# A layer norm between two graph layers, moved from node-major to feature-major

## The reference, cut to what matters

```python
# layer 0, relational: per edge h[src] * norm, summed by (type, dst), times W_rel
W_rel = jnp.einsum('rb,bdf->rdf', w_comp, weight)
agg = jax.ops.segment_sum(h[src] * norm, etype * n_nodes + dst, n_rels * n_nodes)
node_repr = einsum('rnd,rdf->nf', agg, W_rel) + h_bias + h @ loop_weight   # then relu
x = _layernorm(x + _L0_gnn_ref(...))       # (x - mean) / sqrt(var + eps), over 128 features
# layer 1: per edge
e = (x[dst] - x[src]) @ theta_w.T + x[src] @ phi_w.T
e = relu(bn(e)) @ fc1_w.T ;  e = relu(bn(e))
x = _layernorm(x + relu(segment_mean(e, dst) + x))
```

## Time and profile before

| | us |
|---|---|
| median of 3 runs | 3459.71 |
| lowest, highest | 3441.71, 3469.89 |
| the profiled execution, its time | 3434.9 |
| its span | 3433.1 |
| busy PE, DVE, ACT, POOL | 2137.0, 1219.2, 698.3, 1869.4 |
| mean granted PE clock, share of full | 0.719 |

### The profile page before, as it was taken

How to read it: one execution, slowest core, us unless ns; L and a number is a source line. 1 busy time by engine, 2 the same in 40 slices (tenths; PEclk the granted TensorE clock), 3 DMA queues, 4 the chain that set the end, 5 groups by cost and what they waited for, 6 DMA issues and landing times. The chain is left out here.

```text
span 3433.1 us, 51738 instructions
## 1 busy us (share of the span) xinstructions
PE 2137.0 (62%) x11161; PEld 1666.7 (49%) x11162; DVE 1219.2 (36%) x3285; ACT 698.3 (20%) x1046; POOL 1869.4 (54%) x2429
## 2 busy tenths in 40 slices
PE   3665666666666655455455554565555579799992
PEld 2555555556566544233333333333333333599991
DVE  3333333333343355233333332333333367411116
ACT  2111111111111121000000000010000045566661
POOL 5665666666666601555555555555555500499990
PEclk9788777877777867555655555555555599999995
DMA  5122211222122103222222222232222267433331
GB/s 120 50 55 53 54 52 51 57 56 52 52 55 57 46 7 110 71 84 83 83 82 82 82 82 82 82 96 83 75 90 85 78 252 277 157 134 134 134 122 38
DMA packets 120501, 300.17 MB, mean 87 GB/s; under 512 B 34397, under 2 KB 71282, under 8 KB 101632
## 3 DMA queue, kind: packets, MB, share of 16 engines
q1 hardware_dynamic: 63216, 145.36, 12.7%
q0 software_dynamic: 50176, 102.86, 11.7%
q10 hardware_dynamic: 7056, 51.38, 3.8%
HBM read 235.97 MB, written 63.51 MB: 87 GB/s over the span
## 5 line engine op out<-in xcount | busy, mean ns | idle before, releaser
L568 POOL DMA_INDIRECT G<-btab,ix x784 | 739.5, 943 | 639.6 <-POOLq L56 422.9
L554 POOL DMA_INDIRECT G<-in_x,srcT x784 | 746.5, 952 | 461.8 <-issue 230.3
L725 PE MATMUL PS<-BIG,onesb 2*128 2x512 bf16 x196 | 109.8, 560 | 640.5 <-PEq L56 361.6
L659 PE MATMUL PS<-BIG 128*128 128x192 f32 x1568 | 354.2, 373 | 140.1 <-issue 139.6
L650 PE MATMUL PS<-BIG,G 128*128 128x192 f32 x1568 | 366.1, 396 | 85.1 <-PEq L56 41.7
L1274 DVE TENSOR_SCALAR ohT<-PS,node_col 80x512 bf16<-80x512 f32 x196 | 146.1, 745 | 705.8 <-DVEq L56 512.2
L659 PEld LDWEIGHTS PS<-BIG 128*128 128x128 f32 x1568 | 309.6, 221 | 173.1 <-issue 173.1
L734 PE MATMUL PS<-ident,G 128*128 128x128 f32 x1568 | 376.6, 416 | 16.4 <-issue 11.6
L650 PEld LDWEIGHTS PS<-BIG,G 128*128 128x128 f32 x1568 | 333.7, 239 | 100.8 <-issue 99.9
L594 POOL TENSOR_SCALAR BIG<-iota_w,BIG 128x80 f32<-128x80 f32 x784 | 360.7, 481 | 18.6 <-POOLq L56 15.7
L900 ACT ACTIVATE BIG<-PS 128x512 f32<-128x512 f32 x196 | 117.0, 597 | 1220.5 <-ACTq L56 733.2
(11 more groups left out here) (168 smaller groups left out, 1910.1 us busy)
## 6 DMA issues: line engine op xcount, KB each, us to landing
BIG<-spill SPq DMA_DIRECT2D x98, 1024.0 KB, 4.7
spill<-BIG ACTq DMA_DIRECT2D x49, 1024.0 KB
G<-in_x,srcT POOLq DMA_INDIRECT x784
G<-btab,ix POOLq DMA_INDIRECT x784
typ_i<-in_edge_type SPq DMA_DIRECT2D x97, 128.0 KB
BIG<-atab SPq DMA_DIRECT2D x196, 60.0 KB
atab<-BIG SPq DMA_DIRECT2D x13, 384.0 KB, 2.6
btab<-bst SPq DMA_DIRECT2D x13, 256.0 KB, 2.3
```

What stands on the lines that cost most here:

```text
L554: nc.gpsimd.indirect_dma_start(out=G[:, g % 2, t, :], out_offset=None, in_=x, in_offset=bass.IndirectOffsetOnAxis(ap=srcT[:, TPG * g + t:T ...
L568: nc.gpsimd.indirect_dma_start(out=G[:, h, t, :], out_offset=None, in_=rows_of, in_offset=bass.IndirectOffsetOnAxis(ap=ix[:, h, t:t + 1], ...
L659: mm = pe.matmul(PS[:, 4 + p, 0:TPP * TWIN], basis[:, b, :], zs[:, p, :, b, :], start=(b == 0), stop=(b == B - 1), skip_group_check=True)
```

## The change

The norm is done unit by unit and feature-major. Since layer norm is (x - mean) times a number r for each node, and taking the mean off is a product with a constant matrix, B = r * (x C W) for C = identity - 1/128. The kernel makes `ctab` once, the constant C beside both weights times C, and for each unit PE multiplies the feature-major residual by it: that gives centred x and centred B; ACT squares and sums the first for the variance and scales the second by r. The last unit has two windows instead of four. All of B is made and stored before A. POOL waits for B's stores alone. x is loaded window by window in the first pass and kept transposed in `X`'s place; the bias goes in with the loop product. `steps_lo` and `steps_hi` move to another PSUM bank. A root activation stands at ACT's beginning. (Declarations are cut.)

```diff
 SP
-            sp.wait_ge(rows_used, 1)
-            sp.dma_start(X[:, 0:NW - 1, :], x[0:(NW - 1) * TNODES, :].rearrange("(w p) d -> p w d", p=P)).then_inc(x_in, 16)
-            sp.dma_start(X[0:LASTN, NW - 1, :], x[(NW - 1) * TNODES:N, :]).then_inc(x_in, 16)
-            with sp.Fori(1, NC - 1) as c:
-                take(sp, typ_free)
-                load_types(c, [ROW] * TPC)
...
+            def first_pass(g, h, use):
+                take(sp, xw_free)
...
+                    sp.dma_start(xn[:, h, 0:D], x[bass.ds(g * TNODES, TNODES), :]).then_inc(x_in[h], 16)
+                    if h == 0:
+                        take(sp, typ_free)
...
+                            load_types(use + 1, [ROW] * TPC)
...
-            def store_tables(u, s, use):
...
-            sp.sem_inc(tabs_done, 1)
+            def store_b(u, s, use):
+                n = len(windows_of(u))
                 take(sp, bst_ready)
...
+            by_pairs(sp, NBU, store_b)
+            def store_a(u, s, use):
+                n = len(windows_of(u))
                 take(sp, ast_ready)
...
+            by_pairs(sp, NBU, store_a)
 POOL
-            by_pairs(pool, NBU, keep)
-            pool.wait_ge(tabs_done, 1)
+            pool.wait_ge(bst_out[0], 16 * (NBU - NBU // 2))
+            pool.wait_ge(bst_out[1], 16 * (NBU // 2))
             gathers(btab[:, :])
 PE
+            pe.matmul(PS[:, 5, 0:2 * D], center[:, :], thph[:, :], start=True, stop=True).then_inc(cw_ps, 1)
...
-                    take(pe, xwin_ready)
+                    reached(pe, "pe", x_in[h], 16 * (use + 1))
                     take(pe, loop_done)
                     pe.transpose(PS[:, 7, 0:P], xn[:, h, 0:D], ident[:, :]).then_inc(xwT_ps, 1)
...
-            by_pairs(pe, NBU, turn_sums)
-            def node_tables(u, s, use):
...
+            def centred(u, s, use):
+                take(pe, xres_ready)
+                take(pe, cb_free, 2)
+                for w in windows_of(u):
+                    for half in range(2):
+                        mm = pe.matmul(PS[:, 2 * s + half, w * D:(w + 1) * D], ACC[:, bass.ds((u * WPB + w) * TNODES, TNODES)],
+                                       ctab[:, half * D:(half + 1) * D], start=True, stop=True, skip_group_check=True)
+                mm.then_inc(cb_ps, 1)
+            for u in range(NBU):
+                centred(u, u % 2, u // 2)
+            def dst_tables(u, s, use):
+                take(pe, a_free)
...
+                                   ctab[:, 2 * D:3 * D], start=True, stop=True, skip_group_check=True)
+                mm.then_inc(a_ps, 1)
 ACT
+            act.activation(small[:, 60:61], ones[:, 0:1], ACT.Sqrt)
...
-            act.wait_ge(x_in, 32)
-                act.activation(xn[:, h, 0:D], win(X, g), ACT.Copy).then_inc(xwin_ready, 1)
...
                         take(act, xwT_ps)
-                        act.activation(xT[:, h, 0:D], PS[:, 7, 0:P], ACT.Copy).then_inc(xwT_ready, 1)
+                        act.sem_inc(xw_free, 1)
+                        act.activation(XT[:, bass.ds(g * TNODES, TNODES)], PS[:, 7, 0:P], ACT.Copy).then_inc(xwT_ready, 1)
...
-            turned_sums(bn_in[:, 4:5])
-            def copy_b(u, s, use):
...
+            def squares(u, s):
+                take(act, cb_ps)
+                for w in windows_of(u):
+                    v = u * WPB + w
+                    ins = act.activation(square[:, s, w, :], PS[:, 2 * s, w * D:(w + 1) * D], ACT.Square,
+                                         accum_out=ssq[:, bass.ds(v, 1)])
+                ins.then_inc(squares_ready, 1)
+            def src_tables(u, s, use):
+                if not last(u, NBU):
+                    squares(u + 1, 1 - s)
...
+                take(act, var_ready)
+                act.activation(ln_mv[:, at_u, 1], ln_mv[:, at_u, 0], ACT.Sqrt).then_inc(sd_ready, 1)
+                take(act, r_ready)
...
+                for w in range(n):
+                    ins = act.activation(bst[:, s, w * D:(w + 1) * D], PS[:, 2 * s + 1, w * D:(w + 1) * D], ACT.Copy, scale=ln_r[:, bass.ds(u * WPB + w, 1)])
+                ins.then_inc(act_self, 1)
+                take(act, act_self)
+                act.sem_inc(cb_free, 1)
+                act.sem_inc(bst_ready, 1)
+            squares(0, 0)
+            by_pairs(act, NBU, src_tables)
+            def scaled_a(u, s, use):
+                take(act, a_ps)
+                take(act, as_free)
+                for w in windows_of(u):
+                    ins = act.activation(xT[:, s, w * D:(w + 1) * D], PS[:, 4 + s, w * D:(w + 1) * D], ACT.Copy,
+                                         scale=ln_r[:, bass.ds(u * WPB + w, 1)])
...
+            by_pairs(act, NBU, scaled_a)
             for h in range(2):
...
 DVE
+            step(dve.tensor_scalar(center[:, :], ident[:, :], 1.0 / D, None, ALU.subtract))
...
-                    dve.tensor_tensor(acc, acc, PS[:, 7, P:2 * P], ALU.add).then_inc(added, 1)
+                    dve.scalar_tensor_tensor(out=acc, in0=PS[:, 7, P:2 * P], scalar=bn_in[:, 4:5], in1=acc,
+                                             op0=ALU.add, op1=ALU.add).then_inc(added, 1)
...
+            take(dve, cw_ps)
+            dve.tensor_copy(ctab[:, 0:D], center[:, :])
+            dve.tensor_copy(ctab[:, D:2 * D], PS[:, 5, D:2 * D])
+            step(dve.tensor_copy(ctab[:, 2 * D:3 * D], PS[:, 5, 0:D]))
...
+            def residual0(u):
+                cols = bass.ds(u * (WPB * TNODES), len(windows_of(u)) * TNODES)
+                dve.scalar_tensor_tensor(out=ACC[:, cols], in0=ACC[:, cols], scalar=0.0, in1=XT[:, cols],
+                                         op0=ALU.max, op1=ALU.add).then_inc(xres_ready, 1)
+            def normalise0(u, s, use):
...
+                take(dve, squares_ready)
+                step(dve.tensor_scalar(ln_mv[:, at_u, 0], ssq[:, at_u], 1.0 / D, EPS, ALU.mult, ALU.add))
+                dve.sem_inc(var_ready, 1)
+                if not last(u, NBU) and not last(u, NBU - 1):
+                    residual0(u + 2)
+                take(dve, sd_ready)
+                step(dve.reciprocal(ln_r[:, at_u], ln_mv[:, at_u, 1]))
+                dve.sem_inc(r_ready, 1)
+                for w in range(n):
+                    v = u * WPB + w
+                    ins = dve.tensor_scalar(win(X, v), PS[:, 2 * s, w * D:(w + 1) * D], ln_r[:, bass.ds(v, 1)], None, ALU.mult)
+                ins.then_inc(cb_free, 1)
...
             def split_a(u, s, use):
-                if not last(u, NBU):
-                    send_normal(u + 1, 1 - s, use + s)
-                take(dve, a_ps)
+                take(dve, as_ready)
...
-                step(dve.tensor_copy(hi, ps))
-                step(dve.tensor_tensor(res, ps, hi, ALU.subtract))
-                dve.sem_inc(a_split, 1)
+                step(dve.tensor_copy(hi, a_s))
+                step(dve.tensor_tensor(res, a_s, hi, ALU.subtract))
+                dve.sem_inc(as_free, 1)
```

More of the change, by code:

```diff
@@ L362, in by_pairs, with windows_of @@
             body(n - 1, 0, n // 2)
+        def windows_of(u):
+            return range(NW - WPB * u + 1 if last(u, NBU) else WPB)
         def first_use(use):
@@ new lines, in _ @@
+            sp.sem_inc(xw_free, 2)
+            first_pass(0, 0, 0)
+            first_pass(1, 1, 0)
+            with sp.Fori(1, NG // 2 - 1) as i:
+                first_pass(2 * i, 0, i)
+                first_pass(2 * i + 1, 1, i)
+            for g in range(NG - 3, NG):
+                first_pass(g, g % 2, g // 2)
+            def store_b(u, s, use):
+                n = len(windows_of(u))
+                take(sp, bst_ready)
+                sp.dma_start(btab[bass.ds(u * (WPB * TNODES), n * TNODES), :].rearrange("(w p) d -> p w d", p=P),
+                             bst[:, s, 0:n * D].rearrange("p (w d) -> p w d", w=n)).then_inc(bst_out[s], 16)
@@ L854, in copy_z @@
                         take(act, xwT_ps)
-                        act.activation(xT[:, h, 0:D], PS[:, 7, 0:P], ACT.Copy).then_inc(xwT_ready, 1)
+                        act.sem_inc(xw_free, 1)
+                        act.activation(XT[:, bass.ds(g * TNODES, TNODES)], PS[:, 7, 0:P], ACT.Copy).then_inc(xwT_ready, 1)
             by_pairs(act, NG, copy_z)
-            def turned_sums(bias):
-                def copy_sums(u, s, use):
-                    if not first_use(use):
-                        take(act, accw_ps)
-                    act.activation(xT[:, s, :], ACC[:, bass.ds(u * (WPB * TNODES), WPB * TNODES)], ACT.Identity,
-                                   bias=bias).then_inc(accw_ready, 1)
-                by_pairs(act, NBU, copy_sums)
-                take(act, accw_ps, 2)
@@ L954, in _, with copy_sums @@
             by_pairs(act, NG, relu_e2)
-            turned_sums(0.0)
+            def copy_sums(u, s, use):
+                if not first_use(use):
+                    take(act, accw_ps)
+                act.activation(xT[:, s, :], ACC[:, bass.ds(u * (WPB * TNODES), WPB * TNODES)], ACT.Copy).then_inc(accw_ready, 1)
```

(31 more changed lines are left out.)

114 lines of the change are left out of this document (48 added, 66 removed).

## The result

| | before | after |
|---|---|---|
| median of 16 runs each, us | 3455.11 | 3480.72 |
| lowest, highest | 3436.23, 3476.41 | 3460.54, 3494.14 |
| profiled execution, its time (span) | 3434.9 (3433.1) | 3482.75 (3480.9) |

The ratio is 1.0067, 95% interval 1.0044 to 1.0089: slower by 15 to 31 us, where +6.5 was forecast.

The account below looks back on a forecast made before the run. The first pass was taken as held by stalls of instruction supply, the table stage as paid in full. Start -14, tables +25.5 and handover -5 gave +6.5: 3441 us on the profiled execution, 3466 on the median; range 3395 to 3530.

Parts of the forecast that it names:

- Start, -14: First pass's start: dropping the load of all x lets DVE and PE begin earlier; -14 us, ends -18 and -5.
- stalls of instruction supply: First pass: held by these more than by arithmetic; PE loses 139.6 us before the basis product with nothing to wait for.
- Groups, 0: First pass, each group: window loads and smaller ACT work cost 0, ends -1 and +1.5 us a group.
- the rival of +71: First pass: x window loads stall PE, 1.45 us per load issued, +71 us to 3537; chance 0.16.
- the rival of -60: First pass runs nearer POOL's floor: groups fall from 23.4 to 22.2 us, -60 us to 3406; chance 0.20.
- Source tables, 89 with the filling: New source-table stage: 12.5 units at 6.7 us (ends 5.3 and 9) make 84, and 5 to fill.
- The hops between engines: Source tables: signalling from engine to engine in one turn, 0.36, 0.1 and four at 0.15, in all 1.1 us.
- the ring: Source tables: each unit goes serially round PE, ACT and DVE with no step overlapping another; 6.7 us a turn.
- Destination tables, 46: Stage after the source tables: DVE sets 3.5 us a unit; 12.5 units are 44 us, and 2 to fill.
- PE's term: Source tables: PE's 8 products in 16 instructions per unit, 2.68 us; ends 2.0 and twice that.
- Handover, -5: Tables to second pass: the first look-up waits for the window rows alone; -5 us, ends -10 and 0.
- Square and root reload each other's tables: Source tables on ACT: switching functions each unit costs 26 loads of 1.28 us, +33 us to 3499; chance 0.04.

Follow-up runs that it names:

- e0: Kernel before and kernel after, both unedited, run again in a slow session: after 3527.36 us, ratio 1.0049; before 3511.53 us in one run.
- e4: Kernel after with the two loads of all x, ACT's window copies and the wait on them put back; 2827.72 us, ratio 1.0082 to the kernel before.
- e8: Kernel after with ACT's squares of unit u+1 moved behind the scaled copies of unit u; 2795.23 us, ratio 0.9958 to the kernel before.
- e1: Same edit as e8: kernel after, ACT's root and scaled copies of unit u ahead of the squares of u+1; 2792.42 us, ratio 0.9957.
- e5: Kernel after with both the reorder of e1 and the early indices of e3; slow session, 3488.66 us, ratio 0.9934 to the kernel before.
- e3: Kernel after with ACT writing the first two groups' indices ahead of the destination tables; 2807.91 us, ratio 1.0015 to the kernel before.
- e11: Same edit as e3 against the kernel after, first indices written ahead of the destination tables; 2811.22 us, ratio 1.0014 to the kernel before.
- e9: Kernel after without the type loads behind the first lot, so with wrong types; 2823.68 us, ratio 1.0057 to the kernel before.
- e2: Kernel after with POOL waiting, after the first group's 16 gathers, until DVE has scaled the first coefficients; 2825.70 us, ratio 1.0077.
- e7: Same edit as e2 against the kernel after, POOL held until DVE has scaled the first coefficients; 2829.57 us, ratio 1.0079.
- e6: As e5, with DVE also taking the residual of unit u+3 behind its scalings of u; 3492.08 us, ratio 0.9943 to the kernel before.

## Why the prediction was right, and where not

**The forecast held in kind**: little change, slightly slower, from the table stage. The time lies in the range, 3395 to 3530, but that range is 135 us wide, wide enough that a start worth nothing could not throw it out. The sum was 16 us low, 13 of them from one step that failed, the start.

**Start, -14 (ends -18 and -5): wrong, -0.8, and -2.0 in the pair of e0.** PE's first product came at 62.9 against 63.7, and not at 48. Start of the first pass, timeline of the kernel after, answering to the earlier trace rows:

```profile
37.86 1.72 SPq L439 DMA_DIRECT2D typ_i<-in_edge_type  x4
38.11 0.80 PE L653 MATMUL PS<-BIG 128*128 128x32 bf16 x24 [4.26 <-issue]
...
51.80 0.94 POOL L575 DMA_INDIRECT G<-in_x,srcT  x1 [0.30 <-issue]
56.37 0.42 DVE L1100 TENSOR_TENSOR BIG<-PS,normT 128x256 f32<-128x256 f32 x1 [18.75 <-DVEq L56]
...
62.88 4.80 PE L668 MATMUL PS<-BIG,G 128*128 128x192 f32 x16 [22.93 <-PEq L56]
...
66.70 0.94 POOL L575 DMA_INDIRECT G<-in_x,srcT  x1 [13.96 <-POOLq L56]
```

The load of x is gone, and DVE still waits 18.75 us (19.37 before). I had read a delay that stood beside a transfer as its effect. What the load did hold was ACT, and through ACT PE. The same start in the kernel before:

```profile
54.41 0.31 ACT L844 ACTIVATE xn<-X 128x128 f32<-128x128 f32 x1 [12.09 <-issue]
```

From 54.41 on ACT no longer stood in PE's way, but DVE went on at 57.30 only and had scaled one-hots to write before PE could start at 63.68. The longer wait covered the shorter, so taking the load away gave nothing. In a quick session, without DVE's wait, the load's price comes to light: PE starts at 56.1 with it (e4) and at 45.5 to 46.8 without, and 6 to 8 us of that are left at the last addition.

What the row of DVE also shows is that DVE goes on 3.6 us after POOL's run of 32 gathers has ended (52.74 to 56.37). The six traces of slow sessions have 3.0 to 4.3 there, before and after, with and without the bulk load; in quick sessions DVE goes on at 39 to 41 amid the gathers. So the wait stands beside the gathers, in slow sessions alone. That they cause it was not tested.

The prediction's working spoke of stalls of instruction supply. The Trainium skill (Runtime: NRT & Kernel Launch, Instruction fetch mechanics) says that a taken branch out of the window forces a fetch by DMA before execution goes on. The trace speaks against that as the cause here. DMA queues between 38 and 56 us, the kernel after (packets, MB, share of 16 engines):

```profile
## 3 DMA queue, kind: packets, MB, share of 16 engines
q0 software_dynamic: 416, 0.85, 18.6%
q1 hardware_dynamic: 336, 0.59, 11.7%
```

No instruction queue has a packet in the whole of DVE's wait, here and in the other five traces of slow sessions, and over the whole span these queues move the same in both kinds of session (17 and 38 packets, 0.28 and 0.31 MB). The same goes for the first pass, which the prediction took to be held by such stalls. Its queues in the kernel before, 64 to 1214 us, beside PE's 139.6 us of idle time in the earlier trace rows:

```profile
q14 instruction: 14, 0.11, 0.0%
q8 instruction: 2, 0.03, 0.0%
```

Sixteen small packets in 1150 us are few: to make up the 139.6 us, each would have to hold PE for 8.7 us (an estimate).

**Groups, 0 (ends -1 and +1.5 a group): right.** First pass +10.6 in one pair and -14.9 in the other; per group +0.2 and -0.3. The window loads cost nothing that shows, which settles the rival of +71, and the rival of -60 did not come in either slow pair. In a quick session the floor of 20 us a group is met, 968.6 us in e8 over 49 groups. That isn't the change's doing, for the kernel before is as quick there (2804 and 2808 us).

**Source tables, 89 with the filling (6.7 a unit, ends 5.3 and 9): right, 92.4.** The last addition ends at 1257.2, the last scaled copy at 1349.5. A full unit takes 7.3, 0.6 more than forecast, and the start and the half unit at the end take less than was put down for them. Steps of the unit shown, beside what was taken: PE's products to ACT's first square 3.98 (2.68 and a hop), squares with their sums 1.19 (1.3), root to reciprocal 0.46, reciprocal to copies 0.61, copies to the next product 1.40 (1.3 and a hop). The term that was too small is PE's. Groups of the source and destination tables, the kernel after:

```profile
L728 PE MATMUL PS<-ctab,ACC 128*128 128x128 f32 x200 | 44.8, 416 | 48.4 <-PEq L56 48.4
...
L888 ACT ACTIVATE BIG<-PS 128x128 f32<-128x128 f32 x52 | 13.7, 277 | 61.2 <-ACTq L56 61.2
L888 ACT ACTIVATION_READ_ACCUMULATOR BIG<-PS (+1 forms) x52 | 10.7, 206 | 0.0
```

44.8 us over 12.5 units are 3.58 each, at a granted clock of 0.65, where the earlier trace rows gave 2.68 at 0.83. The hops between engines, which the prediction had put at 0.15 each without a row, are 0.2 to 0.4 in the unit shown, and their sum is 1.2 where 1.1 was taken. With ACT's order changed (e1, e5, e8) the same 200 products take 35.0 to 37.4 us at 0.74 to 0.76, against 43.0 to 45.5 in the traces that keep it. So the ring with more idle time in it has the lower clock, and while PE is in the ring the lower clock lengthens it. That the idle time is what lowers the clock was not tested.

**Destination tables, 46: right, 45.4** (1349.5 to 1394.9). Tables together +28.6 for +25.5, the miss being PE's term again, a small one.

**Handover, -5: right, -5.0**, and for the reason given: ACT writes the indices behind its last copy. The handovers of e3, e5 and e11 (8.0, 7.6, 8.0), whose gathers begin 42 to 61 us ahead of the last split's end, show that the look-up's own chain, from the A stores, sets it, and not the gathers.

**Square and root reload each other's tables: no.** The Trainium skill (ScalarE: Activation LUTs, Rules for kernel authors) was quoted for this rival. The kernel after has one load in its whole trace, this one, where the kernel before had two (at 5.46 and 1280.82):

```profile
0.71 1.28 ACT L850 ACT_TABLE_LOAD   x1 [0.71 <-PEq L1463]
```

Squares, roots and scaled copies alternate 13 times without a further load, so they share a set here, and the page's price for a switch has nothing to count. The load alone took 1.28 us.

**The sum.** -14 + 25.5 - 5 = +6.5 became -0.8 + 28.6 - 5.0 = +22.8. The ratio gives 0.0067 x 3455 = 23 us. In the pair of e0 it is -2.0 + 28.6 - 5.1 = +21.5, and the ratio gives 0.0049 x 3509 = 17. That the first agree so well is in part luck: the sum leaves out the two long passes, in which the traces before and after differ by up to 16 us, and the ratio's interval is 15 to 31 us.

**Open.** Why a slow session is slow. The same instructions last the same; engines stand idle while gathers run, and only then (the rest behind the second pass takes 685 to 688 us in both kinds of session, and the tables of the kernel after without gathers 138). Whether type loads add to the stalls in a slow session (e9) and whether a quiet POOL lets DVE go on there (e2, e7) is not known, since these kernels ran in quick sessions. A first pass with fewer gathers was not run. How the reordered ring and the early indices share e5's gain in a slow session is open too.

## What to carry to other kernels

When a step is made unit by unit over several engines, write down the order of each engine's stream and follow one unit round: a step for the next unit placed ahead of this unit's release closes a ring, and here moving two lines took 27 us of 138 away. A consumer's early start is worth nothing while a small input to it, here two index rows, stands behind the work that it was meant to overlap. And before a delay is put down to the transfer beside it, follow the code from the transfer to whoever waits for it, and see whether a longer wait covers that one.

## What the runs showed of the hardware

- The same kernel takes 3455 or 3509 us in some sessions and 2804 or 2808 in others, and one recorded chip number stands for both. The traces differ in one more way: those of slow sessions hold about 20,000 semaphore updates, those of quick ones about 50,000, for the same program. So in a slow session's trace "issue" in a row need not mean that nothing was waited for: the update may be missing (not shown for any single row). I had built on that word.
- An activation from PSUM with a summed output is two instructions on ACT, 277 ns and 206 ns for 128 columns, that overlap: from the first of four pairs to the root took 1.19 us.
- A gather of 128 rows costs POOL 0.94 to 0.95 us and 0.30 of issue in every session. Where B's gathers began beside the destination tables (e3, e5, e6, e11), the first four took 1.18 to 1.28.
- A set of 16 products of 128x128x128 in f32 took 2.02 us at a granted clock of 1.00 (e1, 1028 to 1038 us) and 3.75 at 0.50 (the kernel after, 1282 to 1298).
